# Self-attention stage: maxima by query halves spread around the value products, and the spread q copied from PSUM by ScalarE

## The chip, the cores and the metric

The program runs on one core of a Trainium2 chip. The metric is the device time of one execution in microseconds (us), lower is better. Engines: PE (TensorE, matrix products), DVE (VectorE), ACT (ScalarE), POOL (GpSimd), SP (SyncE, which issues DMAs here). Each works through its own queue in order, and they wait for each other by semaphores.

## The reference, cut to what matters

The program is a model of four layers (attention and mixture-of-experts stages, then an alignment stage and a last one). The change touches one stage, the self-attention of the third mixture layer, on `B, S, H = 2, 1024, 256` with 16 heads of 16 features:

```python
q = (x @ wq.T).reshape(B, S, num_heads, D)      # D = 16, the same for k and v
scores = jnp.einsum('bqhd,bkhd->bhqk', q, k) * scale
probs = jax.nn.softmax(scores, axis=-1)
out = jnp.einsum('bhqk,bkhd->bqhd', probs, v).reshape(B, S, H)
return out @ wo.T
```

## The kernel before, in words

`self_attention` works in 8 units: 4 groups of 4 heads times 2 batches. A unit has 16 steps, 2 query blocks of 512 by 8 key tiles of 128. In a step, PE makes the scores of 4 heads transposed (keys on the partitions, line 1601) in two pairs of banks (0 to 3), ACT takes Exp of one pair at a time into `probs` (line 1656, two of 128x1024 a step), and PE multiplies the probabilities of the step before by the values (`pv`, line 1569) into bank 7, where a block's 8 steps add up. The denominators come out of the same product, from columns of ones in `v_tok`.

The softmax subtracts each query's maximum. It is known before the scores are made, since it is an extra row (`AUX`) of the operand `q_split`, against a row of ones in `k_split`. To get it, PE makes all scores once more with the queries on the partitions, in 64 "pieces" of 128 queries by 512 keys (kind `piece`, line 1556); DVE takes the maximum of each (line 1712); the job `rows` then reduces the halves (line 1685), PE transposes (line 1560), DVE copies the rows to `nmax_rows` (line 1714), and ACT's queue sends them by 4 small DMAs into `q_split` (line 1636). This is all done for unit n+1 while unit n is attended to.

What prepares unit n+1 and what finishes unit n-1 is a list of jobs written into the steps by hand (`schedule`). Each job fills one of three banks (4 to 6, in turn) on PE (`fill`) and is emptied by DVE (`empty`), in the same order; the semaphore `taken` counts the emptied jobs, and PE fills a bank only when the job three places back is taken. The kinds:

- `both` (2): projection of q and k, line 1538; ACT rounds it to `qk_hi` (line 1630), then DVE takes the rest to `qk_lo` (line 1697).
- `spread` (8): q and k of each head brought to their partitions, lines 1543 and 1544. DVE empties all: the four of q at line 1702, the four of k at line 1704.
- `value` (3): the values, line 1549, emptied at line 1707.
- `piece` (64) and `rows` (1), as above.
- `den` (2) and `y_out` (4), of unit n-1: denominators, lines 1531 and 1691, and output product, lines 1535 and 1695. Before `den`, DVE saves bank 7 (`take_values`, line 1676); after it ACT inverts by Ln and Exp (`invert`, lines 1642 and 1644) and DVE multiplies (`divide`, line 1720).

In the schedule before, the pieces lie in steps 2 to 13, two or three pairs a step; step 0 has both `both`; step 1 both `den`, four `spread` and, on ACT, `invert`; steps 2 and 3 two `spread` each; steps 4 and 5 `y_out`; steps 6, 7 and 9 `value`; step 14 `rows`; step 15 nothing. A prologue makes all the jobs of unit 0 but `den` and `y_out`, without attention beside it; the last unit has only `den` and `y_out` beside it, and those of its own follow it.

On PE a step is, in this order: scores of pair 0, up to 2 pieces, scores of pair 1, up to 2 pieces, `pv` of the step before, and the jobs that are left. On ACT: the Exps of a step, then `invert` if the step has it, then the roundings. The scores of a pair wait for the Exp of the same pair one step before. SP reloads the weights of the next group in every other unit.

Of the kernel before, what the change touches and what calls it, by code (L numbers as in the profile page):

```python
# [13 lines left out]
P = 128  # L14
B = 2
# [1375 lines left out]
def self_attention(nc, consts, h, r, t):  # L1391
# [20 lines left out]
    den, y_out, both, spread, value, piece, rows = "den", "y", "both", "spread", "value", "piece", "rows"  # L1412
    VALUES = [range(0, 3), range(3, 6), range(6, KT)]
    Q0, Q1, K0, K1 = 0, 2, 4, 6
    LEAVING = [(den, 0), (den, 1)] + [(y_out, i) for i in range(4)]
    FIRST, PAIRS = 2, PIECES // 2
# [12 lines left out]
    NEXT = [[job for job in jobs if job not in LEAVING] for jobs in schedule]  # L1429
    NJ, NL = sum(map(len, NEXT)), len(LEAVING)  # L1430
    assert NJ % 3 == 0 and NL % 3 == 0, "each unit starts with the same bank"
# [6 lines left out]
    def jobs_of(first, last):  # L1438
        if first:
            return NEXT  # L1440
        return [[job for job in jobs if job in LEAVING] for jobs in schedule] if last else schedule

    def first_job(n, first):

        return NJ if first else (NJ + NL) * n + NJ - NL

    with ExitStack() as stack:
# [9 lines left out]
        q_split = sc.sb("q_split", [P, B, 2, S], F32R)  # L1457
# [5 lines left out]
        nmax_rows = sc.sb("nmax_rows", [NH * KT, P], F32R)  # L1463
        raw = sc.sb("raw", [P, S])
        dens = sc.sb("dens", [P, S])
# [4 lines left out]
        names = """setup placed in_loaded out_loaded job_ps taken hi_ready nmax_ready row_ready  # L1470
# [7 lines left out]
        def cells_of(i):  # L1478

            pair, cell = divmod(i // 2, KT * QB)  # L1480
            return 2 * pair + i % 2, cell // QB, cell % QB
# [12 lines left out]
        def _(sp):  # L1494
# [6 lines left out]
            def reload(g, first):  # L1501

                n, plan = B * g, jobs_of(first, False)
                if not first:
                    sp.wait_ge(s["taken"], first_job(n, False) + place_of((y_out, 3), plan) + 1)
                    load_out(bass.ds(g, 1))
                sp.wait_ge(s["taken"], first_job(n, first) + place_of((value, 2), plan) + 1)
                load_in(slice(1, 2) if first else bass.ds(g + 1, 1))
# [6 lines left out]
            reload(0, True)  # L1515
            with sp.Fori(1, GROUPS - 1) as g:
                reload(g, False)
            last_group = GROUPS - 1
            sp.wait_ge(s["taken"], first_job(B * last_group, False) + place_of((y_out, 3), schedule) + 1)
            load_out(slice(last_group, last_group + 1))  # L1520

        @block.tensor
        def _(pe):
            def fill(kind, i, m, mb, left, base, place, plan=None):
# [3 lines left out]
                bank = ps[:, 4 + place % 3, :]  # L1528
# [22 lines left out]
                elif kind == piece:  # L1551
                    if i == 0:
                        pe.wait_ge(s["taken"], base + place)
                    hd, qt, kb = cells_of(i)
                    rr = rows_of(hd)
                    mm = pe.matmul(bank, q_split[rr, mb, hd // 2, qt * P:(qt + 1) * P],  # L1556
                                   k_split[rr, mb, hd // 2, kb * BLK:(kb + 1) * BLK], start=True, stop=True)
                else:
                    pe.wait_ge(s["nmax_ready"], m + 1)
                    mm = pe.transpose(bank[0:NH * KT, 0:P], nmax[:, :], consts["ident"][:, :])  # L1560
# [13 lines left out]
            def body(n, b, first, last):  # L1574
# [5 lines left out]
                pe.wait_ge(s["row_ready"], 64 * n + 64)  # L1580
                plan = jobs_of(first, last)
                for i, jobs in enumerate(plan):
# [3 lines left out]
                    def pieces(count):  # L1586

                        nonlocal place, done
                        while count and done < len(jobs) and jobs[done][0] == piece:
                            fill(*jobs[done], n + 1, 1 - b, n - 1, base, place, plan)  # L1590
                            place, done, count = place + 1, done + 1, count - 1

                    for pair in range(NH // 2):
# [5 lines left out]
                        for hd in (2 * pair, 2 * pair + 1):  # L1599
                            rr = rows_of(hd)  # L1600
                            pe.matmul(ps[:, hd, :], k_split[rr, b, pair, kt * P:(kt + 1) * P],  # L1601
                                      q_split[rr, b, pair, blk * BLK:(blk + 1) * BLK], start=True, stop=True)\
                              .then_inc(s["score_ps"], 1)
                        pieces(2)
# [21 lines left out]
        def _(act):  # L1626
            def round_both(blk, base, plan):
                place = place_of((both, blk), plan)
                act.wait_ge(s["job_ps"], base + place + 1)
                act.activation(qk_hi[:, blk, :], ps[:, 4 + place % 3, :], ACT.Copy).then_inc(s["hi_ready"], 1)  # L1630

            def send_rows(b, base, plan):
                act.wait_ge(s["taken"], base + place_of((rows, 0), plan) + 1)
                for hd in range(NH):
# [881 lines left out]
```

## Time and profile before

| | us |
|---|---|
| median of 3 runs (4196.6 to 4197.85) | 4197.21 |
| the profiled execution's own time | 4190.63 |
| its span, first to last instruction | 4188.6 |
| PE busy in the span | 3057.8 (73%) |
| DVE busy in the span | 2086.7 (50%) |
| ACT busy in the span | 1488.5 (36%) |
| maxima of the stage's pieces, line 1712, 512 of them | 318.1 |
| Exps of the stage, line 1656, 256 of them | 250.0 |

Busy times are shares of the whole program; the stage that is changed is a part of it, so that the page as a whole does not tell what bounds it. An engine is busy while one of its instructions runs; its waits stand apart.

### The profile page before, as it was taken

The numbers are of one execution on the slowest core, as the hardware profiler recorded it, in microseconds if no ns is written. First come the engines' busy times: TensorE is split into PE (matmuls) and PEld (weight loads), VectorE is DVE, ScalarE is ACT, GpSimd is POOL, SyncE is SP. The second block draws the span as 40 slices with busy tenths as digits, with TensorE's granted clock in tenths as the row PEclk, the third lists the DMA queues.
The fourth block names the chain that finished last, engine by engine and source line by source line (L and its number), as shares of the span: only waits on it lengthen the run. The fifth ranks groups of instructions, "written<-read, shape, count | busy, mean of one in ns | idle before, by whom it ended". The sixth has DMA issues, their size and how long they took to land. (4 is left out here: it accounts for less than half of the span.)

```text
span 4188.6 us, 40949 instructions
## 1 busy us (share of the span) xinstructions
PE 3057.8 (73%) x14046; PEld 1793.9 (43%) x14046; DVE 2086.7 (50%) x3654; ACT 1488.5 (36%) x2034; POOL 1038.2 (25%) x625
## 2 busy tenths in 40 slices
PE   4999999999956585497585888888289510079769
PEld 1555555545436353496352333332279400034344
DVE  3655655556314263375464677674267453721270
ACT  2344444444424233264232344445156210022230
POOL 0355656556621130301131000000400212001110
PEclk7899999999967797698697899998589755579899
DMA  2000000000004100463100000000156225000260
GB/s 86 4 6 2 4 5 5 5 1 4 2 26 154 41 1 15 159 220 132 30 1 10 3 1 5 4 0 2 55 206 217 67 23 59 3 23 31 86 236 20
DMA packets 92591, 204.64 MB, mean 49 GB/s; under 512 B 31145, under 2 KB 65577, under 8 KB 83738
## 3 DMA queue, kind: packets, MB, share of 16 engines
q0 software_dynamic: 18512, 109.48, 7.7%
q1 hardware_dynamic: 70458, 87.07, 7.7%
q10 hardware_dynamic: 3472, 6.16, 0.4%
q8 instruction: 87, 1.43, 0.1%
q14 instruction: 62, 0.51, 0.0%
HBM read 154.41 MB, written 48.01 MB: 48 GB/s over the span
## 5 line engine op out<-in xcount | busy, mean ns | idle before, releaser
L596 POOL TENSOR_TENSOR A_key_sums<-A_key_sums,A_probs 128x1024 f32<-128x1024 f32 (+1 forms) x224 | 526.9, 2371 | 227.7 <-ACT A_probs L489 227.7
L489 ACT ACTIVATE A_probs<-A_banks 128x512 f32<-128x512 f32 (+1 forms) x576 | 329.8, 597 | 386.4 <-PE A_banks L409 384.2
L539 DVE TENSOR_REDUCE A_part_max<-A_banks 128x1 f32<-128x367 f32 x768 | 354.0, 531 | 156.8 <-PE A_banks L330 155.5
L1656 ACT ACTIVATE F_probs<-F_banks 128x1024 f32<-128x1024 f32 x256 | 250.0, 1022 | 316.7 <-PE F_banks L1601 298.7
L1712 DVE TENSOR_REDUCE F_part_max<-F_banks 128x1 f32<-128x512 f32 x512 | 318.1, 683 | 30.5 <-PE F_banks L1556 28.9
L358 PE MATMUL A_banks<-A_probs,A_v_tok 128*64 128x512 f32 x1152 | 278.7, 605 | 0.0
L407 PE MATMUL A_banks<-A_q_one,A_k_one 128*128 128x512 f32 (+1 forms) x576 | 257.0, 446 | 26.3 <-ACT A_probs L489 23.3
L330 PE MATMUL A_banks<-A_k_one,A_q_one 128*128 128x368 f32 x768 | 230.2, 383 | 6.8 <-ACT A_v_tok L469 6.4
L2022 PE MATMUL G_banks<-G_path,G_ctx_rows 77*128 77x512 f32 x16 | 14.0, 1071 | 294.2 <-DMA G_ctx_rows<-in_G_ctx_rows 294.2
L409 PE MATMUL A_banks<-A_q_two,A_k_two 128*128 128x512 f32 (+1 forms) x576 | 228.0, 396 | 0.0
L1556 PE MATMUL F_banks<-F_k_split,F_q_split 64*128 64x512 f32 x512 | 195.1, 502 | 43.5 <-DVE F_part_max L1712 30.8
L161 POOL TENSOR_SCALAR F_r<-F_r,F_ln_w 128x512 f32<-128x512 f32 x16 | 28.8, 1815 | 746.1 <-DVE F_r L126 746.1
L330 PEld LDWEIGHTS A_banks<-A_k_one,A_q_one 128*128 128x128 f32 x768 | 147.3, 192 | 94.5 <-DVE A_part_max L539 58.5
L1569 PE MATMUL F_banks<-F_probs,F_v_tok 128*32 128x512 f32 x1024 | 147.8, 651 | 29.7 <-ACT F_probs L1656 21.4
L407 PEld LDWEIGHTS A_banks<-A_q_one,A_k_one 128*128 128x128 f32 (+1 forms) x576 | 106.8, 185 | 139.2 <-issue 96.1
L1556 PEld LDWEIGHTS F_banks<-F_k_split,F_q_split 64*128 64x128 f32 x512 | 80.3, 196 | 178.3 <-DVE F_part_max L1712 147.9
L284 PE MATMUL A_banks<-g_y,A_wqkv 128*128 128x512 f32 x256 | 120.6, 615 | 30.7 <-DVE A_part_max L579 26.0
L596 POOL TENSOR_TENSOR A_key_sums<-A_probs 128x1024 f32<-128x1024 f32 x32 | 76.0, 2376 | 263.1 <-ACT A_probs L489 263.1
L843 PE MATMUL F_banks<-F_y_hi,F_w_split 128*128 128x256 f32 x736 | 130.8, 291 | 11.8 <-DVE F_w_split L1002 11.8
L843 PE MATMUL D_banks<-D_y_hi,D_w_split 128*128 128x256 f32 x736 | 130.6, 291 | 11.8 <-DVE D_w_split L1002 11.8
L2170 POOL TENSOR_TENSOR H_diff<-H_logits 128x512 f32<-128x512 f32 x32 | 40.5, 1264 | 394.5 <-DVE H_logits L2155 388.9
L2022 PEld LDWEIGHTS G_banks<-G_path,G_ctx_rows 77*128 77x128 f32 x16 | 5.2, 335 | 302.3 <-DMA G_ctx_rows<-in_G_ctx_rows 295.1
(531 smaller groups left out, 6406.6 us busy)
## 6 DMA issues: line engine op xcount, KB each, us to landing
H_w<-in_H_w SPq DMA_DIRECT2D x16, 1024.0 KB, 7.6
moe_in<-A_zeros ACTq DMA_DIRECT2D x1, 5888.0 KB, 17.4
D_tile_in<-moe_in SPq DMA_DIRECT2D x23, 256.0 KB, 5.3
moe_out<-D_z SPq DMA_DIRECT2D x23, 256.0 KB, 4.9
F_tile_in<-moe_in SPq DMA_DIRECT2D x23, 256.0 KB, 5.3
moe_out<-F_z SPq DMA_DIRECT2D x23, 256.0 KB, 4.9
slots<-H_staged SPq DMA_DIRECT2D x8, 512.0 KB, 3.5
made<-H_made POOLq DMA_DIRECT2D x16, 256.0 KB, 6.8
```

Of the source, the lines that this page charges most:

```text
L330: pe.matmul(ps[:, MAX_BANKS[i % 3], 0:PW], q_one[:, b, j, qt * P:(qt + 1) * P], k_one[:, b, j, (i % 3) * PIECE:(i % 3) * PIECE + PW], star ...
L358: mm = pe.matmul(ps[DH * j:DH * j + DH, 4 + blk, :], v_tok[:, b, kt, DH * j:DH * j + DH], probs[:, j, kt % RING, blk * BLK:(blk + 1) * BLK ...
L407: pe.matmul(ps[0:kw, half % 3, :], k_one[:, b, j, kt * P:kt * P + kw], q_one[:, b, j, cols], start=True, stop=False)
L409: pe.matmul(ps[0:kw, half % 3, :], k_two[:, b, j, kt * P:kt * P + kw], q_two[:, b, j, cols], start=False, stop=True).then_inc(s["score_ps" ...
L489: act.activation(probs[0:kw, j, kt % RING, blk * BLK:(blk + 1) * BLK], ps[0:kw, half % 3, :], ACT.Exp, scale=1.0 / 8.0).then_inc(s["exp_re ...
L539: dve.tensor_reduce(part_max[:, i // 3, i % 3:i % 3 + 1], ps[:, MAX_BANKS[i % 3], 0:PIECE], AX.X, ALU.max).then_inc(s["piece_max"], 1)
L596: pool.tensor_tensor(key_sums[0:kw, j, :], before, probs[0:kw, j, kt % RING, :], ALU.add).then_inc(s["summed"], 1)
L843: mm = pe.matmul(ps[:, 1 + pairs * (n % 2) + pair, at * SLOT:(at + 1) * SLOT], weight_in(i, w_part, pair, c, QM * q + at), part[:, i % 2, ...
L1556: mm = pe.matmul(bank, q_split[rr, mb, hd // 2, qt * P:(qt + 1) * P], k_split[rr, mb, hd // 2, kb * BLK:(kb + 1) * BLK], start=True, stop= ...
L1569: mm = pe.matmul(ps[V0 * hd:V0 * hd + V0, 7, :], v_tok[:, b, kt, V0 * hd:V0 * hd + V0], probs[:, i % RING, hd, :], start=kt == 0, stop=kt ...
L1656: act.activation(probs[:, i % RING, heads_at, :], ps[:, heads_at, :], ACT.Exp, scale=DH ** -0.5).then_inc(s["exp_ready"], 1)
L1712: op = dve.tensor_reduce(part_max[:, hd * KT + qt, kb:kb + 1], bank, AX.X, ALU.max)
```

## The change

- **Pieces by query halves.** A unit's pieces are ordered by query half (the two blocks of 512 queries), 32 each, 4 in every step. Of those of unit n+1, the first half and 8 of the second are made in steps 6 to 15 of unit n (kind `piece`, 40); the other 24 in steps 0 to 5 of unit n+1 itself (kind `now`).
- **Two `rows` jobs.** `(rows, 0)` in step 14 for the first half of the next unit, `(rows, 1)` in step 6 for the second half of this one. PE waits for the rows at steps 0 and 8. Each is sent by 2 DMAs, by SP in place of ACT's queue; `q_split` is laid out by half. On SP these stand in one line with the reloads of the weights.
- **The order on PE:** scores of pair 0, 2 pieces, scores of pair 1, `pv`, 2 pieces, the other jobs.
- **The other jobs are spread:** `both` in steps 0 and 1, `den` 2, `spread` 3 (q), 4 (k), 5 (q), 6 (k), `y_out` 7 and 9, `value`, now 5 jobs of 2, 2, 2, 1 and 1 key tiles, in 10, 11, 12, 13 and 8. `invert` in step 3, `divide` in step 5; bank 7 is saved at step 0.
- **The spread q on ACT.** The four `spread` jobs of q are copied by ACT (`copy_q`, after the Exps and `invert` of their step); DVE waits for the copy and writes one element (`passed`) to count the job as taken.
- The prologue makes 40 pieces in place of 64; the last unit makes 24 and a `rows` job.

```diff
-    VALUES = [range(0, 3), range(3, 6), range(6, KT)]
+    VALUES = [range(0, 2), range(2, 4), range(4, 6), range(6, 7), range(7, KT)]
...
-    for i in range(PAIRS):
-        schedule[FIRST + i * (STEPS - 4) // PAIRS] += [(piece, 2 * i), (piece, 2 * i + 1)]
-    others = {0: [(both, 0), (both, 1)],
-              1: [(den, 0), (den, 1), (spread, Q0), (spread, Q0 + 1), (spread, K0), (spread, K0 + 1)],
-              2: [(spread, Q1), (spread, Q1 + 1)], 3: [(spread, K1), (spread, K1 + 1)],
-              4: [(y_out, 0), (y_out, 1)], 5: [(y_out, 2), (y_out, 3)],
-              6: [(value, 0)], 7: [(value, 1)], 9: [(value, 2)], STEPS - 2: [(rows, 0)]}
+    for i in range(HALF + EARLY, PIECES):
+        schedule[(i - HALF - EARLY) // EACH].append((now, i))
+    HALF_STEPS = HALF // EACH
+    for i in range(HALF + EARLY):
+        schedule[HALF_STEPS - 2 + i // EACH].append((piece, i))
+    schedule[HALF_STEPS - 2].append((rows, 1))
+    schedule[STEPS - 2].append((rows, 0))
+    others = {0: [(both, 0)], 1: [(both, 1)], 2: [(den, 0), (den, 1)], 3: [(spread, Q0), (spread, Q0 + 1)],
+              4: [(spread, K0), (spread, K0 + 1)], 5: [(spread, Q1), (spread, Q1 + 1)], 6: [(spread, K1), (spread, K1 + 1)],
+              7: [(y_out, 0), (y_out, 1)], 9: [(y_out, 2), (y_out, 3)]}
+    for k in range(len(VALUES)):
+        others[10 + k if k < 4 else 8] = [(value, k if k < 4 else 4)]
...
-    DIVIDE_AT = 3
+    INVERT_AT, DIVIDE_AT = 3, 5
...
+            def send_rows(m, b, half, base, plan):
+
+                sp.wait_ge(s["taken"], base + place_of((rows, half), plan) + 1)
+                for j in range(2):
+                    row, mine = AUX + HR * j, HALF // QB // 2
+                    sp.dma_start(q_split[row:row + 1, b, half].bitcast(F32).rearrange("o p (t n) -> o (p t) n", n=P),
+                                 nmax_rows[j * mine:(j + 1) * mine, half, :].bitcast(F32)).then_inc(s["row_ready"], 16)
...
-                        pieces(2)
+                        if pair == 0:
+                            pieces(EACH // 2)
...
+            def copy_q(i, m, b, base, plan):
+                o, blk = divmod(i, QB)
+                place = place_of((spread, i), plan)
+                act.wait_ge(s["job_ps"], base + place + 1)
+                act.activation(q_split[:, b, blk, o, :], ps[:, bank_at(place, plan), :], ACT.Copy).then_inc(s["q_copied"], 1)
...
-                    if (den, 0) in jobs:
+                    if i == INVERT_AT and not first:
                         invert(n - 1, base, plan)
                     for kind, index in jobs:
                         if kind == both:
                             round_both(index, base, plan)
+                        elif kind == spread and index < K0:
+                            copy_q(index, n + 1, 1 - b, base, plan)
...
+                if kind == spread and i < K0:
+                    dve.wait_ge(s["q_copied"], K0 * m + i + 1)
+                    dve.memset(passed[0:1, i:i + 1], 0.0).then_inc(s["taken"], 1)
+                    return
...
-                    if i < K0:
-                        op = dve.tensor_copy(q_split[:, mb, o, cells], bank)
```

## Rows read from the trace of the kernel before

**Rows 1.** Windows: start:end us, length, busy us by engine, PE clock; stages and units
```profile
2268.60:2334.55 65.95, 54.69 (x121) 28.20 (x121) 48.13 (x80) 1.20 (x2) 0.00 (x0) 0.60 0.00 1
2334.55:2402.79 68.24, 59.62 (x314) 24.85 (x314) 48.61 (x80) 32.66 (x34) 0.00 (x0) 0.97 0.02 5
2402.79:2481.06 78.27, 67.44 (x330) 27.20 (x327) 54.43 (x88) 37.02 (x38) 0.00 (x0) 0.94 0.00 1
2481.06:2559.42 78.36, 67.87 (x329) 27.45 (x325) 54.43 (x88) 37.02 (x38) 0.00 (x0) 0.94 0.02 6
2873.64:2918.80 45.16, 38.52 (x200) 11.24 (x196) 6.75 (x9) 35.10 (x37) 0.00 (x0) 0.88 0.00 0
```
**Rows 2.** Windows of unit 2: steps 0-1, 2-5, 6-13 and 14-15
```profile
2481.06:2494.44 13.38, 12.03 (x41) 5.06 (x38) 4.68 (x8) 7.51 (x9) 0.00 (x0) 0.84 0.00 0
2494.44:2517.01 22.57, 19.76 (x87) 7.31 (x87) 20.33 (x32) 9.78 (x10) 0.00 (x0) 1.00 0.00 1
2517.01:2550.54 33.53, 30.34 (x171) 13.80 (x170) 28.59 (x48) 15.84 (x16) 0.00 (x0) 0.95 0.05 13
2550.54:2559.42 8.88, 5.74 (x37) 1.28 (x33) 0.82 (x3) 3.88 (x4) 0.00 (x0) 0.86 0.01 3
```
**Rows 3.** Lines of unit 2: count, busy us, mean ns, idle before and its releaser
```profile
L1656 ACT ACTIVATE F_probs<-F_banks 128x1024 f32<-128x1024 f32 x32 | 31.3, 1022 | 36.3 <-PE F_banks L1601 33.8 <-issue 2.5
L1702 DVE CAST F_q_split<-F_banks 128x512 fp32r<-128x512 f32 x4 | 2.6, 681 | 0.0
L1697 DVE TENSOR_TENSOR F_qk_lo<-F_banks,F_qk_hi 128x512 fp32r<-128x512 f32 x2 | 1.4, 691 | 12.9 <-ACT F_qk_hi L1630 12.9
L1549 PE MATMUL F_banks<-F_w_in,F_r 128*128 128x128 f32 x32 | 4.9, 308 | 0.0
```
**Rows 4.** Timeline of steps 11 and 12, unit 2: start us, us, engine, line
```profile
2539.82 0.50 PE L1601 MATMUL F_banks<-F_q_split,F_k_split 64*128 64x512 f32 x2
2540.16 0.40 PE L1556 MATMUL F_banks<-F_k_split,F_q_split 64*128 64x512 f32 x2
2540.59 2.48 DVE L1712 TENSOR_REDUCE F_part_max<-F_banks 128x1 f32<-128x512 f32 x4 [0.46 <-PE F_banks L1556]
2541.76 1.06 PE L1569 MATMUL F_banks<-F_probs,F_v_tok 128*32 128x512 f32 x8
2542.75 0.50 PE L1556 MATMUL F_banks<-F_k_split,F_q_split 64*128 64x512 f32 x2
2543.29 3.68 DVE L1712 TENSOR_REDUCE F_part_max<-F_banks 128x1 f32<-128x512 f32 x6 [0.21 <-PE F_banks L1556]
```
**Rows 5.** Timeline around the end of unit 2
```profile
2552.84 2.61 ACTq L1636 DMA_DIRECT2D F_q_split<-F_nmax_rows  x4
2557.56 1.94 PE L1569 MATMUL F_banks<-F_probs,F_v_tok 128*32 128x512 f32 x8 [2.95 <-ACT F_probs L1656]
2560.57 5.27 PE L1538 MATMUL F_banks<-F_r,F_w_in 128*128 128x512 f32 x8
2565.88 0.60 ACT L1630 ACTIVATE F_qk_hi<-F_banks 128x512 fp32r<-128x512 f32 x1 [1.12 <-PE F_banks L1538]
```
**Rows 6.** Timeline of ACT and DVE, step 1 of unit 2
```profile
2487.93 1.94 ACT L1656 ACTIVATE F_probs<-F_banks 128x1024 f32<-128x1024 f32 x2
2489.89 1.28 ACT L1642 ACT_TABLE_LOAD   x1
2494.24 1.28 ACT L1644 ACT_TABLE_LOAD   x1
2495.53 1.06 ACT L1644 ACTIVATE F_rden<-F_logden 128x1024 f32<-128x1024 f32 x1
```
**Rows 7.** Timeline at the end of the prologue
```profile
2290.39 9.66 DVE L1712 TENSOR_REDUCE F_part_max<-F_banks 128x1 f32<-128x512 f32 x16
2329.04 0.22 DVE L1685 TENSOR_REDUCE F_nmax<-F_part_max 128x32 f32<-128x64 f32 x1
2329.82 0.28 DVE L1714 CAST F_nmax_rows<-F_banks 32x128 fp32r<-32x128 f32 x1 [0.56 <-PE F_banks L1560]
2330.13 3.24 ACTq L1636 DMA_DIRECT2D F_q_split<-F_nmax_rows  x4
2334.55 1.22 PE L1601 MATMUL F_banks<-F_q_split,F_k_split 64*128 64x512 f32 x4 [4.78 <-DMA F_q_split<-F_nmax_rows]
```
**Rows 8.** Lines of DVE: the shortest instruction shown, one element a partition
```profile
L2249 DVE RECIPROCAL H_share<-H_total 128x1 f32<-128x1 f32 x16 | 2.5, 154 | 0.0
```

More of the change, by code:

```diff
@@ L1409, in self_attention @@
     PIECES = NH * KT * QB
-    den, y_out, both, spread, value, piece, rows = "den", "y", "both", "spread", "value", "piece", "rows"
-    VALUES = [range(0, 3), range(3, 6), range(6, KT)]
+    den, y_out, both, spread, value, piece, now, rows = "den", "y", "both", "spread", "value", "piece", "now", "rows"
+    VALUES = [range(0, 2), range(2, 4), range(4, 6), range(6, 7), range(7, KT)]
     Q0, Q1, K0, K1 = 0, 2, 4, 6
+    EACH = PIECES // STEPS
+    HALF = PIECES // 2
+    EARLY = 2 * EACH
     LEAVING = [(den, 0), (den, 1)] + [(y_out, i) for i in range(4)]
-    FIRST, PAIRS = 2, PIECES // 2
@@ L1425, in self_attention @@
+    for k in range(len(VALUES)):
+        others[10 + k if k < 4 else 8] = [(value, k if k < 4 else 4)]
     for i, jobs in others.items():
         schedule[i] += jobs
-    DIVIDE_AT = 3
-    NEXT = [[job for job in jobs if job not in LEAVING] for jobs in schedule]
-    NJ, NL = sum(map(len, NEXT)), len(LEAVING)
-    assert NJ % 3 == 0 and NL % 3 == 0, "each unit starts with the same bank"
+    INVERT_AT, DIVIDE_AT = 3, 5
+    AHEAD = (both, spread, value, piece)
+    NEXT = [[job for job in jobs if job[0] in AHEAD or job == (rows, 0)] for jobs in schedule]
@@ L1432, in self_attention @@
+    NOW = [[job for job in jobs if job[0] == now or job == (rows, 1)] for jobs in schedule]
+    NN, NW, NL = (sum(map(len, plan)) for plan in (NEXT, NOW, [LEAVING]))
+    ALL = NN + NW + NL
+    assert ALL % 3 == 0, "each unit starts with the same bank"
     UNITS = GROUPS * B
@@ L1438, in jobs_of, with bank_at @@
     def jobs_of(first, last):
-        if first:
-            return NEXT
-        return [[job for job in jobs if job in LEAVING] for jobs in schedule] if last else schedule
+        return [[job for job in jobs if not (first and job in LEAVING) and not (last and (job[0] in AHEAD or job == (rows, 0)))]
+                for jobs in schedule]
     def first_job(n, first):
-        return NJ if first else (NJ + NL) * n + NJ - NL
+        return NN if first else ALL * n + NN - NL
+    def bank_at(place, plan):
+        shift = 0 if plan is NEXT else NN
+        return 4 + (shift + place) % 3
     with ExitStack() as stack:
@@ L1527, in fill @@
                     pe.wait_ge(s["taken"], base + place - 2)
-                bank = ps[:, 4 + place % 3, :]
+                bank = ps[:, bank_at(place, plan), :]
                 if kind == den:
@@ L1612, in body @@
                     for place, (kind, i) in enumerate(LEAVING):
-                        fill(kind, i, None, None, n, base + NL, place)
+                        fill(kind, i, None, None, n, base + NL + NW, place, NEXT)
             pe.wait_ge(s["setup"], 64)
@@ L1629, in round_both @@
                 act.wait_ge(s["job_ps"], base + place + 1)
[L1630 to L1634, printed above, removed]
-                    row = AUX + HR * (hd % 2)
-                    act.dma_start(q_split[row:row + 1, b, hd // 2, :].bitcast(F32).rearrange("o (t n) -> o t n", n=P),
-                                  nmax_rows[hd * KT:(hd + 1) * KT, :].bitcast(F32)).then_inc(s["row_ready"], 16)
+                act.activation(qk_hi[:, blk, :], ps[:, bank_at(place, plan), :], ACT.Copy).then_inc(s["hi_ready"], 1)
+            def copy_q(i, m, b, base, plan):
[3 more added lines that the diff above has]
+                act.activation(q_split[:, b, blk, o, :], ps[:, bank_at(place, plan), :], ACT.Copy).then_inc(s["q_copied"], 1)
             def invert(n, base, plan):
@@ L1668, in _ @@
                 round_both(blk, 0, NEXT)
-            send_rows(0, 0, NEXT)
+            for i in range(K0):
+                copy_q(i, 0, 0, 0, NEXT)
             units(act, body)
@@ L1723, in body @@
                 base, place = first_job(n, first), 0
-                for step, jobs in enumerate(jobs_of(first, last)):
+                plan = jobs_of(first, last)
+                for step, jobs in enumerate(plan):
+                    if step == 0 and not first:
+                        take_values(n - 1, QB - 1)
                     if step == DIVIDE_AT and not first:
```

103 lines of the change are left out of this document (58 added, 45 removed).

## The prediction

> **What bounds the kernel now.** I read the windows of the stage first, then those of one unit, then its lines, then its timeline. The prologue takes 65.95 us, unit 0 68.24, and a full unit 78.3; the first scores of units 1 and 7 stand at 2402.79 and 2873.64 us, so units 1 to 6 take 470.85 us, 78.48 each [rows 1]. Inside a full unit no engine is full: DVE is busy 54.43 us, ACT 37.02, PE 67.9, which holds half-clock stretches and matmuls that wait in the pipeline [rows 1]. The reader should see where DVE rests. In steps 0 and 1 it is busy 4.68 of 13.38 us, in steps 14 and 15 0.82 of 8.88, but 20.33 of 22.57 in steps 2 to 5 and 28.59 of 33.53 in 6 to 13 [rows 2]. So two thirds of a unit run at DVE's pace and the rest, with no pieces in it, is a chain through PE and ACT: ACT's queue spends 2.61 us on the four DMAs, PE rests 2.95 us for the Exps behind them, its clock falls, the next value product takes 1.94 us where it took 1.06, and two `both` take 5.27 us [rows 4, 5]. DVE waits 12.9 us for the roundings [rows 3]. That is the time the change can take back: 24 us of a unit in which DVE rests.
>
> **DVE's work in a unit after.** 54.43 us [rows 1], less the four casts of q, 2.6 [rows 3], plus a second reduction and copy of rows, 0.22 + 0.28 [rows 7]. Two more `value` evictions cost their fixed part; the shortest DVE row is 0.15 us [rows 8], so 0.3. The four one-element writes are not in this trace; between 0 and 0.15 each [rows 8]; I take 0.1, 0.4 in all. Sum 53.0 us.
>
> **PE's work after.** Scores and pieces come in pairs 0.34 us apart (2539.82 to 2540.16), and a value product takes 1.0 (2541.76 to 2542.75) [rows 4]: 4 x 0.34 + 1.0 = 2.4 a step, 38 in 16. Of the others, a `both` is at least 1.7 at the full clock (half of 5.27 is 2.6, and most of that was at half clock [rows 5]), two are 3.4; I put `den`, `y_out` and `spread` at 9 together from the same pace and `value` at 4.3, under its 4.9 [rows 3]. About 55 us. PE and DVE are near each other, so neither hides the other wholly.
>
> **Where DVE will rest.** Per full unit:
> - The pause at `invert`. In step 3 `copy_q` stands behind `invert` on ACT, 2 x 1.28 + 2 x 1.06 = 4.7 us [rows 6], and DVE stands behind `copy_q` for the first job, with everything else queued behind that; both q jobs hold a bank, so PE can fill one more piece and then stands too. When the Exps end DVE still has about 1 us of maxima. So 4.7 + 0.6 for the copy (the price of a rounding [rows 5]) + 0.1 - 1.0 = 4.4, and 0.4 more for the second copy: 4.8. What is late next is PE's refill, perhaps at half clock after its rest, as after the 2.95 us before [rows 5]: 0.3 to 3, I take 1.3.
> - Two `both`: after the last maximum is filled PE needs 1.7, ACT 0.6, a hand-over 0.1; DVE has 1.2 left: 1.2 each, 2.4.
> - Two `rows`: 0.56 for the transposition [rows 7] and 0.3 to refill: 1.8 (0.9 in all if the refill is hidden by the copy; 1.5 each at most, as in step 14 of a unit now).
> - The gap at each value product, 0.21 and 0.46 where steps have only pieces [rows 4]: 0.3 in some 12 steps, 3.6.
> - `den`, `y_out` (3 steps) and the five `value`: 0 to 0.8 each, I take 0.4, 3.0. The second q copies, in step 5, where no `invert` is ahead: 0.5. The last value product of a unit, with its Exp and the saving of bank 7: 1.2.
>
> Together 18.6 us, and a unit 53.0 + 18.6 = 71.6 us in place of 78.48: 6.9 less, 41 us over units 1 to 6. Bounds: with 0.2 at the value products, nothing at `den`, `y_out` and `value`, and the low refill, 66; with 0.46, 0.8, 1.5 and the refill at 3, all at once, 80.
>
> A rule weighs against the pause. The rows show the second table load start 0.02 us after an activation (2494.24) and its successor 1.29 us later [rows 6]. The Trainium skill ("ScalarE: Activation LUTs", What ACT_TABLE_LOAD costs) has each switch of table at a 1.28 us load plus a drain of 1.38 us. By that rule, as an estimate from the page, the pause would be 2.8 us longer and the gain over seven units 19 us smaller. The load agrees with the trace; the drain does not show here, so the sum goes by the rows.
>
> **Rows by SP.** `(rows, 1)` is copied near the end of step 6 and needed at step 8, over 5 us later; `(rows, 0)` near the start of step 15 and needed about 3.4 later. Now the way from the copy (2330.10) to the first score (2334.55) is 4.45 us, of which four issues are 3.24 [rows 7]; with two issues at 0.65 each [rows 5] it is about 2.8. So both are hidden, the second with little to spare. If that cover is gone, say by the weight reload ahead of it on SP in units 1, 3 and 5, it costs a microsecond or two each. ACT gets back 2.61 us a unit [rows 5] and gives 4 x 0.6: ACT is then busy 39 of 72 and is no bound.
>
> **Prologue.** Of the 64 maxima at 9.66 / 16 = 0.60 us [rows 7], 24 leave the prologue and 4 more fall behind the `rows` job, under its DMA: 28 x 0.60 = 16.9. The shorter way of the rows 1.3. The `value` jobs, cut finer, leave DVE less to wait: 0.6. The q copies by ACT, one after the other with DVE waiting, against 0.64 each by DVE: 0.6 more. Sum -18.2; bounds -14 (no gain but the 24 maxima) and -20.
>
> **Unit 0** has no leaving jobs: DVE's work is 54.43 - 48.61 = 5.8 less [rows 1], the pause shrinks to the copies (4.3 less), there is no slow refill (1.3) and no wait for `den` and `y_out` (1.2). 71.6 - 12.6 = 59.0, against 68.24: -9.2.
>
> **The last unit** takes 45.16 us now, with DVE busy 6.75 [rows 1]. It gets 24 maxima, but its steps 0 to 5 are long anyway: `invert` and the Exps of steps 3 and 4 make 4.7 + 2 x 1.94 = 8.6 us [rows 6]. Steps 0 to 2 become 3.3 + 2.8 + 4.4, 3 and 4 8.7, 5 4.0: 23.2; the other ten, at ACT's 2.0 with two `y_out` of 3.6 and one `rows` of 2.4, 24.0. 47.2, +2.0, between 0 and +6. The tail after it is the same.
>
> **Sum.** -18.2 - 9.2 - 41.4 + 2.0 = -66.8. The profiled execution took 4190.63 us, 2.03 more than its span, and would take 4123.8; the median of the runs is 4197.21, 6.6 higher, and I forecast on its scale: 4197.21 - 66.8 = 4130.
>
> **The rivals.**
> - *DVE's rest is only moved.* Lockstep over three banks costs more with two kinds of job in every step: each step keeps what a mixed step has now, and the pause comes on top. For it: in steps 2 to 13 now DVE rests 7.2 us of 56.1 [rows 2], with pieces alone or nearly so; against it: there are three pairs in many of those steps, and two after. With most of the high bounds a unit is 78: 6 x 0.5 + 3 for unit 0 + 18.2 - 4 for the last = 20 us less, 4177. Chance 0.12.
> - *PE fills everything in time.* The gaps at value products, `den`, `y_out`, `value` and the refill go (3.6 + 3.0 + 1.3 = 7.9): 63.7 a unit, 6 x 14.8 + 15 + 18.2 - 1 = 121 less, 4076. Against it: PE's 55 us in 64, in order, beside a pause of 5. Chance 0.08.
> - *The clock stays low after the pause* (the other side). PE stands some 4.5 us in step 4 and falls to half clock, and its work per step, then up to 4.8 + 2 to 3.4 for `spread`, `y_out` or `both`, leaves it waiting on nobody but itself. If steps 4 to 9 run so, each takes about 6.8 in place of 4.8, 12 more: a unit of 84. 6 x 5.5 = 33 more, unit 0 even, prologue -18: 4212. It decides from a unit of 82 up. For it: now the clock falls after a rest of 2.95 us [rows 5], and the prologue, with PE on single pieces, runs at 0.60 [rows 1]. Against it: now it is back by the second `both`, and steps 2 to 5, as full as those, run at 1.00 [rows 2]. The Trainium skill ("TensorE: Matmul & The Clock Gate", HAM oscillation — how this bites in real kernels) tells of a kernel that falls to the low clock in every iteration because each has a wait in it; the rows agree as to one fall a unit. Chance 0.05.
> - *The change doesn't do what it says*, the q copies sitting on ACT in front of Exps that PE waits for. ACT has 35 us to spare; it would only add to the pause. No case of its own.
>
> **How the numbers follow.** Forecast 0.75, rivals 0.12, 0.08 and 0.05. About 0.2% (8 us) is what a measurement can tell from no change. The range goes from 4095 (units of 66, 33 us under the forecast) to 4177, the first rival's figure. Faster 0.92: the prologue and unit 0 are nearly sure; same 0.03, between the first rival and the third; slower 0.05.
>
> **What would show it.** In the profile after: full units 71 to 72 us apart; DVE busy near 53 in each; a single rest of DVE of about 5 us a unit, in step 3, released by ACT's q copy; no rest of 12 us for the rounding; the prologue near 48 us and unit 0 near 59; mean clock of a unit 0.9 or more. Wrong if DVE's rest is spread evenly over all steps at over 1.3 us each, if PE waits for the rows' DMA at step 0, or if the clock in steps 4 to 9 is 0.6.

## Result and profile after

| | before | after |
|---|---|---|
| median us | 4196.91 (4192.85 to 4197.85) | 4143.76 (4139.58 to 4149.49) |
| profiled execution, its span | 4190.63, 4188.6 | 4139.58, 4137.5 |

The ratio of after to before is 0.9874, 95% interval 0.986 to 0.9889: 53 us less, where 67 were forecast (4130). It lies in the range given and on the side given. The last kernel of the experiments had one more execution, of 12542.25 us, beside five of 4109.34 to 4119.19; nothing here explains it, and every figure leaves it out.

The windows of the kernel after, cut as in [rows 1]: the prologue, unit 0, units 1 to 6, the last unit. Columns as there: stretch, length, busy us (count) of PE, PEld, DVE, ACT and POOL, granted PE clock, DMA share, GB/s.

```profile
2271.60:2317.62 46.02, 40.00 (x97) 21.14 (x97) 31.38 (x58) 3.47 (x6) 0.00 (x0) 0.61 0.01 3
2317.62:2383.18 65.56, 60.67 (x314) 24.66 (x314) 47.54 (x85) 34.71 (x38) 0.00 (x0) 0.90 0.02 5
2383.18:2455.65 72.47, 64.02 (x330) 26.08 (x326) 53.26 (x93) 38.82 (x42) 0.00 (x0) 0.93 0.00 1
2455.65:2527.05 71.40, 63.29 (x331) 25.76 (x327) 53.21 (x93) 38.85 (x42) 0.00 (x0) 0.95 0.02 7
...
2599.23:2674.47 75.24, 65.31 (x330) 26.16 (x326) 53.45 (x93) 39.02 (x42) 0.00 (x0) 0.91 0.02 6
...
2819.34:2865.97 46.63, 40.88 (x225) 13.19 (x221) 22.10 (x35) 35.31 (x37) 0.00 (x0) 0.93 0.00 1
```

Units 1 to 6 take 436.16 us from first scores to first scores (2383.18 to 2819.34), 72.69 each, in place of 78.48. The ledger against [rows 1]: prologue -19.9, unit 0 -2.7, units 1 to 6 -34.7, last unit +1.5, together -55.8. The span fell by 51.1, so the rest of the program took 4.7 more; of that 3.0 stands ahead of the stage, which none of the edits touches. The start of the stage lay between 2266.8 and 2277.6 us in the kernels run here, so I take the 5 us outside it for scatter of executions.

The waits of DVE in unit 2 of the kernel after: what it waited for, us in total, times, the longest.

```profile
DVE F_part_max L1756 <- PE F_banks L1598: 7.8, 13, 1.6
DVE F_passed L1732 <- ACT F_q_split L1680: 5.3, 4, 4.1
DVE F_qk_lo L1744 <- ACT F_qk_hi L1674: 3.0, 2, 1.5
```

The 12.9 us that DVE waited for the two roundings [rows 3] are 3.0. In their place stands a new wait, for ScalarE's q copies, 5.3 us, of which 4.07 are one pause. The timeline of unit 2 around it, PE's weight loads left out (start us, us, engine, line; in brackets the idle time ahead and its releaser):

```profile
2471.47 1.28 ACT L1685 ACT_TABLE_LOAD   x1
2472.77 1.06 ACT L1685 ACTIVATE F_logden<-F_dens 128x1024 f32<-128x1024 f32 x1
2472.77 0.50 PE L1644 MATMUL F_banks<-F_q_split,F_k_split 64*128 64x512 f32 x2
2473.11 0.39 PE L1598 MATMUL F_banks<-F_k_split,F_q_split 64*128 64x512 f32 x1
2473.84 1.28 ACT L1687 ACT_TABLE_LOAD   x1
2475.14 1.06 ACT L1687 ACTIVATE F_rden<-F_logden 128x1024 f32<-128x1024 f32 x1
2476.10 1.06 ACT L1680 ACTIVATE F_q_split<-F_banks 128x512 fp32r<-128x512 f32 x2
2476.73 0.06 DVE L1732 MEMSET F_passed<- 1x1 f32 x1 [4.07 <-ACT F_q_split L1680]
2476.84 0.50 PE L1598 MATMUL F_banks<-F_k_split,F_q_split 64*128 64x512 f32 x1 [3.35 <-DVE F_passed L1732]
...
2477.50 1.58 PE L1611 MATMUL F_banks<-F_probs,F_v_tok 128*32 128x512 f32 x8
```

One engine passes the pause to the next: ACT inverts from 2471.47 until it can start the copies at 2476.10, DVE stands behind the copy queued there, PE has filled the last free bank at 2473.11 and stands until DVE's write at 2476.73. Then the clock falls, as after the rest in [rows 5]: from 2479 to 2481 the granted clock is 0.50, which is 1.2 GHz, and the value product takes 1.58 us in place of 1.06.

The windows of the same unit by steps: 0 to 3, 4, 5 to 7, 8 to 13, 14 and 15.

```profile
2455.65:2472.76 17.11, 16.28 (x76) 6.33 (x72) 13.29 (x22) 10.02 (x11) 0.00 (x0) 1.00 0.00 1
2472.76:2481.57 8.81, 5.46 (x21) 2.04 (x20) 3.14 (x7) 6.20 (x7) 0.00 (x0) 0.81 0.00 1
2481.57:2497.24 15.67, 13.72 (x62) 5.24 (x61) 12.06 (x22) 6.96 (x8) 0.00 (x0) 0.89 0.00 1
2497.24:2518.74 21.50, 21.36 (x135) 10.07 (x134) 18.41 (x32) 11.71 (x12) 0.00 (x0) 1.00 0.02 8
2518.74:2527.05 8.31, 6.46 (x43) 2.08 (x42) 6.31 (x13) 3.96 (x4) 0.00 (x0) 1.00 0.13 35
```

Step 4, which begins with the scores at 2472.77, takes 8.81 us where its neighbours take 3.8 and 4.5. The reader should also look at PE: outside steps 4 to 7 and 14 and 15 it is busy nearly all the time (16.28 of 17.11, 21.36 of 21.50) and DVE is not (13.29, 18.41). So with the pieces spread, most steps go at PE's pace.

The low clock of the third stretch is not in the steps next to the pause. Steps 6 and 7 alone:

```profile
2486.08:2491.39 5.31, 3.71 (x22) 1.67 (x21) 3.51 (x9) 2.54 (x4) 0.00 (x0) 1.00 0.00 0
2491.39:2497.24 5.85, 5.85 (x21) 1.90 (x20) 4.15 (x7) 2.00 (x2) 0.00 (x0) 0.71 0.01 1
```

Step 5 has the full clock too, and in step 6 PE rests again, for the maxima that `rows` needs. These are PE's two large waits of units 1 to 6 (us in total, times, the longest):

```profile
PE F_banks L1598 <- DVE F_passed L1732: 20.1, 6, 3.4
PE F_banks L1602 <- DVE F_nmax L1727: 19.6, 12, 1.7
```

### The profile page after: what moved, and what is told of

Its sections match the earlier page's. It is cut to its first block and busy times, and to the rows that moved or that the text cites. A ratio compares the mean times of both kernels' runs of the same rounds, so it can differ in the third digit from the quotient of the medians.

```text
span 4137.5 us, 41106 instructions
## 1 busy us (share of the span) xinstructions
PE 3030.0 (73%) x14054; PEld 1782.1 (43%) x14054; DVE 2077.2 (50%) x3686; ACT 1504.2 (36%) x2066; POOL 1037.3 (25%) x625
## 5 line engine op out<-in xcount | busy, mean ns | idle before, releaser
L1598 PE MATMUL F_banks<-F_k_split,F_q_split 64*128 64x512 f32 x512 | 159.5, 499 | 30.5 <-DVE F_passed L1732 20.3
L1644 PE MATMUL F_banks<-F_q_split,F_k_split 64*128 64x512 f32 x512 | 133.6, 476 | 4.9 <-ACT F_probs L1697 4.4
```

The lines of the kernel that those rows point to most:

```text
L1598: mm = pe.matmul(bank, q_split[rr, b, qt * P // BLK, hd // 2, qt * P % BLK:qt * P % BLK + P], k_split[rr, b, hd // 2, kb * BLK:(kb + 1) * ...
```

## Experiments

Times are medians of four or five runs. The ratio is to the kernel before, run beside each group on the same chip (4197.21 us for the first four, 4194.13 for the next four, 4193.75 for the last two). A single unit can be a microsecond or two off the mean of its kernel, so both are given.

| kernel | us | ratio, 95% | length of unit 2 | mean of units 1 to 6 |
|---|---|---|---|---|
| after, again | 4138.99 | 0.9859, 0.9844 to 0.9874 | 71.62 | 72.39 |
| after, q before the inversion | 4129.87 | 0.9841, 0.9827 to 0.9854 | 69.97 | 70.95 |
| after, q on VectorE | 4107.47 | 0.9791, 0.9778 to 0.9804 | 65.89 | 67.18 |
| before, q on ScalarE | 4232.01 | 1.0077, 1.0064 to 1.0091 | 85.03 | 84.21 |
| after, no tables | 4106.02 | 0.9794, 0.978 to 0.9807 | 67.81 | 68.20 |
| q on VectorE, rows in the middle | 4085.0 | 0.974, 0.9727 to 0.9754 | 64.01 | 64.41 |
| q on VectorE, pieces before values | 4133.52 | 0.9855, 0.984 to 0.987 | 71.64 | 71.56 |
| q on VectorE, rows sent by ACT | 4125.16 | 0.9825, 0.9809 to 0.9841 | 70.6 | 70.53 |
| after, q of step 3 on VectorE | 4109.34 | 0.9795, 0.9782 to 0.9807 | 68.28 | 68.17 |
| after, rows in the middle | 4112.02 | 0.981, 0.9798 to 0.9823 | 68.56 | 69.63 |

### The change taken apart: q back on VectorE, and q on ScalarE alone

On the kernel after, the four q tiles go back to VectorE and `copy_q` goes:

```diff
-                        elif kind == spread and index < K0:
-                            copy_q(index, n + 1, 1 - b, base, plan)
...
-                if kind == spread and i < K0:
-                    dve.wait_ge(s["q_copied"], K0 * m + i + 1)
-                    dve.memset(passed[0:1, i:i + 1], 0.0).then_inc(s["taken"], 1)
-                    return
...
+                    if i < K0:
+                        op = dve.tensor_copy(q_split[:, mb, blk, o, :], bank)
```

> The new schedule alone, with the spread q evicted by DVE as before. Queue theory: the pause goes as in the run before (2.7 us in 6 units), and DVE gets 2.3 us more work a unit, of which perhaps half shows, since DVE rests 18 us a unit: 5 us less than the changed kernel, between 15 less and 8 more. Rival (DVE's load is what the copies by ACT relieved, and the pause costs nothing): 2.3 us x 7 = 16 us more than the changed kernel.

4107.47 us, 31.5 less than the kernel after in the same group, or 28.5 by the two ratios; some 30. That half of the change costs time, and several times what I expected. The windows of this kernel, unit 2, cut by steps as above:

```profile
2452.61:2469.74 17.13, 16.30 (x76) 6.32 (x73) 13.45 (x23) 10.03 (x12) 0.00 (x0) 1.00 0.00 1
2469.74:2474.13 4.39, 4.09 (x22) 1.53 (x21) 3.94 (x7) 4.36 (x5) 0.00 (x0) 1.00 0.01 2
2474.13:2488.74 14.61, 12.82 (x62) 5.01 (x63) 13.03 (x22) 6.56 (x7) 0.00 (x0) 1.00 0.01 2
2488.74:2510.18 21.44, 21.29 (x135) 10.04 (x134) 18.39 (x32) 11.73 (x12) 0.00 (x0) 1.00 0.02 7
2510.18:2518.50 8.32, 6.47 (x44) 2.08 (x43) 6.31 (x13) 3.97 (x4) 0.00 (x0) 1.00 0.11 33
```

Step 4 takes 4.39 us in place of 8.81 (-4.4) and steps 5 to 7 14.61 in place of 15.67 (-1.1, as step 7 has the full clock here); all else is the same to 0.1 us. Over units 1 to 6 step 4 takes 26.4 us in place of 54.9. That is 28.5 of the 33.1 us between the two kernels there; 20.1 of it is PE's wait shown above, and the other 8.4 lie in the same step, at a granted clock of 0.63 to 0.81. DVE is busy 55.1 us a unit here, 1.9 more, and no step of unit 2 is longer by more than 0.3 us: where I had priced DVE's time as the unit's, PE's chain covered it.

The counterpart, on the kernel before: its schedule is kept, and only `copy_q` with the one-element write is added (`copy_q` behind `invert`, as in the change).

```diff
+                        elif kind == spread and index < K0:
+                            copy_q(index, n + 1, 1 - b, base, plan)
...
+                if kind == spread and i < K0:
+                    dve.wait_ge(s["q_copied"], K0 * m + i + 1)
+                    dve.memset(passed[0:1, i:i + 1], 0.0).then_inc(s["taken"], 1)
+                    return
```

> The kernel before, with only the spread q copied by ACT. There the two q jobs of step 1 also stand behind the inversion. Queue theory: the evictions of step 1 and the maxima of step 2 come 3.5 us later in units 1 to 6, and DVE has 2.3 us less to do later in the unit: 5 to 20 us more than the kernel before. Rival (relieving DVE pays wherever it stands): 2.3 x 7 = 16 us less than the kernel before.

4232.01 us, 35 slower than before, above the range I gave. The timeline of its step 1 shows the same chain of waits on the other schedule:

```profile
2507.44 1.06 ACT L1652 ACTIVATE F_rden<-F_logden 128x1024 f32<-128x1024 f32 x1
2508.40 1.07 ACT L1637 ACTIVATE F_q_split<-F_banks 128x512 fp32r<-128x512 f32 x2
2509.03 0.06 DVE L1701 MEMSET F_passed<- 1x1 f32 x1 [4.00 <-ACT F_q_split L1637]
2509.14 0.50 PE L1544 MATMUL F_banks<-F_qk_hi,F_place_hi_lo 128*128 128x512 f32 x1 [3.32 <-DVE F_passed L1701]
```

The 4.00 us of DVE and 3.32 of PE stand where the copy of 1.28 for two tiles stood. From first scores to first scores, step 1 takes 10.56 us against 7.1 before, step 2 8.03 against 5.89, step 3 7.27 against 6.23: 6.6 a unit. Steps 2 and 3 run at a granted clock of 0.57 and 0.76 here, and at 1.00 in the kernel before. So the two halves of the change add: the new order of the work brings about 90 us (4197 to 4107), the q copies by ScalarE take some 30 of them back.

### Is it the queue behind the inversion?

First, the copies are put ahead of the inversion in ScalarE's order:

```diff
-                    if i == INVERT_AT and not first:
-                        invert(n - 1, base, plan)
                     for kind, index in jobs:
...
                             copy_q(index, n + 1, 1 - b, base, plan)
+                    if i == INVERT_AT and not first:
+                        invert(n - 1, base, plan)
```

> In step 3 ACT copies the two q jobs before it inverts. Queue theory (DVE's rest of 4.1 us in step 3 comes from the copy standing behind the inversion in ACT's queue, and PE's half clock after it from that rest): steps 3 and 4, now 12.6 us, shrink to about 10, where the Exps behind the inversion hold PE; 2.7 us in each of 7 units, 16 to 20 us less than the changed kernel. Rival (PE's own pace sets a unit now, 63 us of work in 72, and the rest is absorbed by it): within 5 us of the changed kernel.

4129.87 us, 9 less than the kernel after (8 by the ratios) and half of what I expected. ScalarE in that kernel:

```profile
2470.34 0.60 ACT L1680 ACTIVATE F_q_split<-F_banks 128x512 fp32r<-128x512 f32 x1 [0.58 <-PE F_banks L1585]
2471.19 0.60 ACT L1680 ACTIVATE F_q_split<-F_banks 128x512 fp32r<-128x512 f32 x1 [0.25 <-PE F_banks L1585]
2471.80 1.28 ACT L1685 ACT_TABLE_LOAD   x1
...
2475.47 1.06 ACT L1687 ACTIVATE F_rden<-F_logden 128x1024 f32<-128x1024 f32 x1
2476.43 1.92 ACT L1697 ACTIVATE F_probs<-F_banks 128x1024 f32<-128x1024 f32 x2
...
2477.49 0.50 PE L1644 MATMUL F_banks<-F_q_split,F_k_split 64*128 64x512 f32 x2 [2.50 <-ACT F_probs L1697]
```

The long wait of DVE is gone, but ScalarE waits 0.58 and 0.25 us for the q tiles and starts the inversion only then, 0.7 us behind the first scores of step 4 (2471.08) where it was 1.3 ahead of them. So the Exps of step 4 come late and PE stands 2.50 us for them; step 4 takes 6.41 us and step 5, at a clock of 0.69, 5.6. The pause was moved to another waiter.

Then the inversion is made cheap: its Ln and Exp become two plain copies, which load no table. This kernel leaves the inverse of the denominators out; all else is as in the kernel after.

```diff
-                act.activation(logden[:, :], dens[:, :], ACT.Ln).then_inc(s["logden_ready"], 1)
+                act.activation(logden[:, :], dens[:, :], ACT.Copy).then_inc(s["logden_ready"], 1)
-                act.activation(rden[:, :], logden[:, :], ACT.Exp, scale=-1.0).then_inc(s["rden_ready"], 1)
+                act.activation(rden[:, :], logden[:, :], ACT.Copy).then_inc(s["rden_ready"], 1)
```

> The changed kernel, q copied by ACT behind the inversion, but with Copy in place of Ln and of Exp in the inversion, so that ACT loads no table there (the division is by a wrong factor; all else is computed as before). Queue theory (what the q copies by ACT cost is the length of the inversion that stands ahead of them, 4.7 us with its two loads, 2.1 without): step 4, now 8.8 to 9.7 us, becomes about 6.3, 2.6 us in each of units 1 to 6, and a low clock or two less: 16 to 24 us under the changed kernel (4120, ratio to before about 0.981). Rival (the copies cost by themselves, by the hand-over from ACT to DVE wherever they stand): the loads are in nobody's way, under 6 us.

4106.02 us, 27 less than the kernel after by the ratios (0.9794, 0.9859), with the copies still behind it:

```profile
2466.02 1.06 ACT L1685 ACTIVATE F_logden<-F_dens 128x1024 f32<-128x1024 f32 x1
...
2468.08 1.06 ACT L1680 ACTIVATE F_q_split<-F_banks 128x512 fp32r<-128x512 f32 x2
2468.71 0.06 DVE L1732 MEMSET F_passed<- 1x1 f32 x1 [1.36 <-ACT F_q_split L1680]
```

Without the 2.56 us of table loads DVE's pause falls from 4.07 to 1.36 us and step 4 from 8.81 to 4.95, now at the full clock. Part of the gain isn't the pause: the last unit shortened too, where the inversion stands ahead of Exps that PE waits for (step 4 there 3.33 us against 6.04).

Last, the sharpest test: VectorE copies only the two tiles of step 3, those behind the inversion; ScalarE keeps the two of step 5.

```diff
-                        elif kind == spread and index < K0:
+                        elif kind == spread and Q1 <= index < K0:
```

> VectorE copies the two q tiles of step 3, the ones that come behind the inversion; ScalarE still copies the two of step 5, where nothing of the inversion is ahead of it. Theory (the price is the queue behind the inversion, not the copies): the step behind the inversion falls to about 4.4 us from 8.8, the unit takes 66 to 67 us, and the time is that of the version with all four copies on VectorE, 4107 to 4112, some 30 under the kernel after. Rival (each copy by ScalarE costs a hand-over through a second engine, wherever it is): half of the 31 us comes back, 4122 to 4126.

4109.34 us, as with all four on VectorE (ratios 0.9795 and 0.9791, each within the other's interval; units 1 to 6 of the two traces are 6.0 us apart). The windows of steps 4 and 5 to 7 of its unit 2, and its waits of DVE there:

```profile
2472.64:2477.03 4.39, 4.09 (x22) 1.53 (x21) 3.94 (x7) 4.36 (x5) 0.00 (x0) 1.00 0.00 2
2477.03:2492.67 15.64, 13.85 (x61) 5.56 (x62) 12.22 (x22) 7.65 (x9) 0.00 (x0) 0.89 0.00 1
```
```profile
DVE F_passed L1732 <- ACT F_q_split L1680: 0.8, 2, 0.5
```

Step 4 is the 4.39 us of the kernel with all four on VectorE. The two copies by ScalarE with nothing long ahead of them make DVE wait 0.8 us in all, and steps 5 to 7 take 1.0 us more than with all four on VectorE (15.64, 14.61), with the clock at 0.89. Without any pause in step 4 they are as long and at the same clock as in the kernel after (15.67, 0.89), so what they lose there is not the pause. The rival, a fixed price for the hand-over wherever it is, would have kept half of the 30. By the medians 2 us of it are left and by the traces 6, so at least four fifths of the price is the place in ScalarE's queue.

### What sets the rest of a unit

But for the second, these start from the version with q on VectorE. The first two move the `rows` jobs, which stand behind all pieces of their step; there PE waits 1.60 us for the maxima, in the kernel after and in that version. The kernel after:

```profile
2490.11 0.28 PE L1602 MATMUL F_banks<-g_ident,F_nmax 128*16 128x128 f32 x1 [1.60 <-DVE F_nmax L1727]
```

```diff
-    schedule[HALF_STEPS - 2].append((rows, 1))
-    schedule[STEPS - 2].append((rows, 0))
+    schedule[HALF_STEPS - 2].insert(2, (rows, 1))
+    schedule[STEPS - 2].insert(2, (rows, 0))
```

> The new schedule with q evicted by DVE, and each `rows` job put after the first two pieces of its step in place of after all four, so that DVE reduces the halves while PE makes the value product. PE-order theory (once the pause is gone a unit is set by PE's own chain, 61 us busy in 66, and each wait of PE counts in full): PE's wait for the reduction, 1.6 us twice a unit, falls to 0.3 to 0.9; 1.8 us a unit, 10 to 18 us under the same kernel without the edit (4107, ratio 0.979), so 4090 to 4097. Rival (DVE, 55 us busy in 66, sets the steps around it, and PE waits for a bank instead): within 5 us of 4107.

4085.0 us, the fastest here, 0.974 of before. It and the kernel on which it builds were timed in different groups; by the ratios to before, 0.974 and 0.9791, the gain is 21. The transposition in step 6 of its unit 2, and the windows of the unit and of step 6:

```profile
2466.78 0.28 PE L1602 MATMUL F_banks<-g_ident,F_nmax 128*16 128x128 f32 x1 [0.29 <-DVE F_nmax L1723]
```
```profile
2437.99:2502.00 64.01, 61.66 (x330) 24.99 (x327) 54.87 (x93) 36.74 (x38) 0.00 (x0) 1.00 0.03 7
2464.23:2468.94 4.71, 4.31 (x23) 1.62 (x23) 4.16 (x9) 1.94 (x2) 0.00 (x0) 1.00 0.00 1
```

PE's wait falls from 1.60 to 0.29 us; step 6 from 5.57 to 4.71, step 14 from 4.77 to 3.01, while step 15 goes from 3.55 to 4.02. PE is busy 61.66 of 64.01 us, at the full clock.

The wait for the maxima also bears on the clock. Cut step by step, the kernel after runs step 7 at 0.71 to 0.78 in all six full units, and step 15 at 0.65 in one. With only q of step 3 on VectorE it is step 7 in four units and step 15 in five, with q on VectorE step 7 in one and step 15 in three. A low step 15 takes 4.8 to 4.9 us, another 3.6. With the rows in the middle neither step is ever below 1.00, here and in the next kernel, which has the pause. So what is lost behind step 4 hangs on this wait. Why the clock falls behind it in six units of the kernel after and in one with q on VectorE is not shown; the pause alone is not it, since step 7 is low in four units without one. In unit 2 with q of step 3 on VectorE, PE rests 1.60 us, starts again at 2485.64, and then has half clock:

```profile
2486.20:2487.20 1.00, 1.00 (x4) 0.66 (x2) 0.34 (x2) 0.00 (x0) 0.00 (x0) 0.50 0.00 0
```

Is that gain independent of the pause? The same two lines on the kernel after, q left on ScalarE:

> The kernel after, q copied by ScalarE as there, with both `rows` jobs placed after the first pair of pieces of their step instead of behind the last. Theory (the two are independent: one is in steps 6, 7, 14, 15, the other in steps 4 to 8): the gain seen with q on VectorE, 22 us, comes here too, 4115 to 4119. Rival (step 6 and 7 already run at a low clock behind the pause, so less or more comes back there): a gain of 10 to 15, 4124 to 4129, or of 30 and more if the earlier rest was what kept the clock low.

4112.02 us, 21 less than the kernel after by the ratios (0.981, 0.9859): the gain comes whole. Step 4 of its unit 2 still takes 8.8 us at a clock of 0.81, and steps 5 to 7 behind it have the full clock. The versions with and without q on ScalarE lie 0.007 of the ratio apart here as there.

PE's order in a step, put back to two pieces behind each pair of scores, ahead of the value product:

```diff
-                        if pair == 0:
-                            pieces(EACH // 2)
+                        pieces(EACH // 2)
```

> The new schedule with q evicted by DVE, but with both pairs of pieces ahead of the value product as in the kernel before, in place of one ahead and one behind. PE-order theory: PE waits for a bank ahead of the value product, then DVE has nothing left behind it: 0.3 to 0.5 us a step, 5 to 8 us a unit, 35 to 55 us more than 4107. Rival (the order is worth nothing, PE's work is the same and three banks bridge it): within 8 us.

4133.52 us, by the ratios (0.9855, 0.9791) 27 slower, less than I expected; unit 2 takes 71.64 us in place of 65.89. Steps 10 to 12 take 4.02 us each in place of 3.40, 3.53 and 3.53, steps 1 and 2 5.42 in place of 4.59 and 4.68, and step 5 6.93 in place of 4.59, where PE waits 1.18 us for a bank and the clock is 0.75. The last three (3.58, 3.73 and 3.8 in place of 3.07, 4.77 and 3.55) gave a little back.

The rows sent by ScalarE's queue as before, two DMAs each, ahead of the Exps of the next step:

```diff
-                    sp.dma_start(q_split[row:row + 1, b, half]...
+                    act.dma_start(q_split[row:row + 1, b, half]...
```

> The new schedule with q evicted by DVE, and the rows sent from ACT's queue as before, two DMAs a half, in place of SP's. PE-order theory: in step 15 the Exps start 1.3 us later, and the last value product of the unit waits for them, 1.3 us a unit; in step 7 it is hidden: 7 to 12 us more than 4107. Rival (ACT, 37 us busy in 66, has room everywhere): within 4 us.

4125.16 us, by the ratios (0.9825, 0.9791) 14 slower than q on VectorE, a little above what I expected, and the runs scattered more (4110 to 4137). Step 0 takes 6.19 us in place of 4.02, at a granted clock of 0.52; so it is in units 2, 4, 5 and 6, while it has the full clock in 1 and 3. What the low clock alone costs there I didn't separate.

Of the 90 us that the new order brings, these two parts, taken back one at a time, are worth 27 and 14. The rest, above all the pieces in steps 0, 1, 14 and 15, where DVE rested before, was not tried by itself.

## Why the prediction was right, and where it was not

**The right side and near size.** 4143.76 against 4130. The term that made most of it held: a unit, forecast at 71.6 us, took 72.7; DVE's work, 53.0, took 53.2; its rest in unit 2 was 71.40 - 53.21 = 18.2, forecast 18.6 (unit 2 is the shortest of the six; in the mean of them it is 19.4). The pause at `invert`, forecast as 4.8 for both jobs, was 4.07 + 0.43 = 4.5, and the copies of step 5 cost 0.82 where 0.5 were put (2 x `F_passed`, 0.28 and 0.54). The two `both` were 3.0, forecast 2.4. `rows` by SP were hidden, and the write of one element is 0.06 us, not 0.1. The prologue came out at -19.9 (-18.2), the last unit at +1.5 (+2.0; its ten last steps add up to 23.6, not 24.0).

**Unit 0 is the term that was mis-sized,** 65.56 against 59.0: 6.5 us less gain than forecast, where the stage's ledger missed by 11.0 in all (units 1 to 6 another 6.7, the prologue and the last unit 2.2 the other way). I took away DVE's work on the leaving jobs (5.8), a wait for them (1.2), the pause (4.3) and the refill (1.3). The last two are nearly right: q on VectorE takes a full unit to 67.2 in the mean, 65.9 in unit 2, and I would have had it at 71.6 - 4.8 - 1.3 = 65.5. The leaving jobs, 7.0 with the wait, look nearly right too: against that unit 2, steps 2, 7 and 9 of unit 0 are 2.5, 1.2 and 1.9 us shorter (2.23, 3.23, 3.03 against 4.68, 4.45, 4.94), 5.6 in all. What I left out is what gives it back. Its step 0 starts at the prologue's low clock, runs at 0.50 throughout and takes 6.43 us in place of 4.02:

```profile
2317.62 0.80 PE L1644 MATMUL F_banks<-F_q_split,F_k_split 64*128 64x512 f32 x2 [0.59 <-DMA F_q_split<-F_nmax_rows]
...
2320.34 3.78 PE L1579 MATMUL F_banks<-F_r,F_w_in 128*128 128x512 f32 x4
2324.05 0.62 PE L1644 MATMUL F_banks<-F_q_split,F_k_split 64*128 64x512 f32 x2
```

The first `both` takes 3.78 us; 1.7 was my price for one at the full clock, where it takes 1.98. Steps 3, 8 and 10, at the full clock, are 0.8, 0.7 and 0.7 longer than in that full unit. Each stands right behind one of the three short steps, so 2.2 of the 5.6 us go to the next step: in step 3 PE's pieces wait for DVE, which reduces six in a row (3.67 us from 2329.99). The same three lengths stand in unit 0 of the versions with q on VectorE. Of the 7.0 that I took off for the leaving jobs, 3.4 came. Step 15 is 1.3 longer, at a clock of 0.64, as after the wait for the maxima in some full units.

**Units 1 to 6** are 1.1 us longer each than forecast, 6.7 in all. 3.1 of that is one of them, the unit of 75.24 us, beside a mean of 72.2 of the others; with q on VectorE the long one stands at the same place (69.11 against 66.8). It begins with a stall of DVE of 1.92 us for which the profile shows no releaser. It is unit 4, the first of the second pass of the loop over groups (units 2 and 3, then 4 and 5), and all ten traces of the new order have the stall there, of 1.88 to 2.17 us, while before the same instruction in their other full units it waits 1.5 at most. That it belongs to the loop is likely, and not shown.

**A wrong reading behind a right sum.** I built a unit as DVE's work plus DVE's rests. In the parts this fails: a load of 2 us more on DVE moved nothing (q on VectorE), while PE's order alone (pieces before values) moved 4.4 in the mean, low clock included. The term behind it is PE's work, which I put at 55 us: with the rows in the middle, at the full clock, PE is busy 61.7. My 9 for `den`, `y_out` and `spread` is 2.0 + 4.0 + 7.2 = 13.2 there, two `both` are 4.0 and not 3.4, `value` is 4.9 and not 4.3. That PE's chain with this error and my sum of DVE's rests came to nearly the same unit is in part luck. My rival "PE fills everything in time" had a unit at 63.7; the version with the rows in the middle takes 64.4 in the mean, and the two things between it and the kernel after are the pause (5.5) and the wait ahead of the two `rows` (2.8), with the low clock that each brings. I had put 1.8 on the latter, as DVE's rest, and thought half of it could be hidden at most; what counted was PE's, 1.60 twice, and two places earlier in the step it goes nearly whole.

**The rival "the clock stays low"** had the right cause and too long a reach: step 4 ran at 0.63 to 0.81 in the six full units, step 5 was back at 1.00, and the low clock of step 7 hangs on the wait for the maxima. It cost 1.4 us a unit in step 4 beside PE's wait, not 12. My reading of the rows, one fall a unit, was also short by one: cut step by step, units 1 to 6 of the kernel before have a second low clock in step 9 (0.76), hidden in the 0.95 of [rows 2]. The Trainium skill ("TensorE: Matmul & The Clock Gate", HAM oscillation — how this bites in real kernels) tells of a kernel that falls to the low clock in every iteration. The trace agrees: step 4 is below 1.00 in each of the six full units.

**"The change doesn't do what it says"** was dismissed with the sentence that ScalarE has 35 us to spare. That was the fault with the largest price, though it stands in no term: it does as it says, but this half of the change is a loss of some 30 us. I had the 4.8 + 1.3 us of the pause in the ledger and never set them against what the relief of DVE buys.

## What to carry to other kernels

Before moving an eviction to an engine with time to spare, read what stands ahead of it in that engine's queue at that step, and who holds a buffer until it is done: 4.7 us of inversion ahead of two copies cost some 30 us in the whole stage, and the two other copies, with nothing long ahead, 1 us a unit at most. Find out which engine paces the steps before pricing relief: here PE's order did, and 2 us less on DVE bought nothing. Look also for a job that needs the last result of its step: put last, it makes PE wait, and the clock can fall behind the wait (21 us here for moving two lines). A change of two halves can hide a loss in a gain; the sum of the path should be made for each half alone.

## What the runs showed of the hardware

- A table load is 1.28 us and its activation starts 0.02 us behind it (2473.84, 2475.14); the drain of 1.38 us that the Trainium skill ("ScalarE: Activation LUTs", What ACT_TABLE_LOAD costs) adds to a switch of table does not show. The same page of the Trainium skill (Table sets: the hidden batching unit) has Ln and Exp in one set, so that Ln and then Exp need one load; here there are two in each inversion, one at Ln and one at Exp. As an estimate from the measured load, one less would shorten the pause by 1.28 us; that was not tried.
- Two loads less (2.56 us) took 3.9 us from step 4, which ran at 1.00 and no longer at 0.81: this pause cost its length and the low clock behind it.
- Behind a rest of PE of 1.60 us the granted clock was 0.50 (2486.20, q of step 3 on VectorE). That was so in some units of a trace and not in others with the same rest.
- A one-element write by DVE takes 0.06 us, and PE's matmul follows it 0.11 us later (2476.73, 2476.84), so the hand-over of a count by such a write is cheap when nothing is queued ahead of it.
